# Window attention stage of a fused kernel: when the values are projected, in which PSUM bank, and the order of three small steps around it

## The chip, the cores and the metric

The kernel runs on one core of one Trainium2 chip. The metric is the device time of one execution in microseconds; lower is better. All times below are of the kernel before the change.

## The reference

Four images of 128 channels and 112 x 112 pixels pass two blocks with a residual each, `x = x + L0(gn(x))` and `x = x + L1(gn(x))`, where `gn` is a group norm over 32 groups of 4 channels. The change touches the first block only:

```python
win = (windows of 8 x 8 pixels: 64 tokens of 128 channels)
xn = (win - mu) * rsqrt(var + eps) * ln_gamma + ln_beta     # layer norm over the channels
q, k, v = split(xn @ w_qkv.T + b_qkv)                       # 8 heads of 16
attn = softmax((q * scale) @ k.T)                           # 64 x 64 for each window and head
o = (attn @ v) @ w_out.T + b_out
```

The second block is a linear attention over the whole image with a depthwise 3 x 3 convolution, and an MLP of 1024 hidden channels with the exact GELU. Its inputs need the group norm of what the first block wrote.

## The kernel before

All of it is one program. In the attention stage (the profile's first 1,080 us or so) an image of 112 x 112 lies in SBUF as `ximg` and is worked through in 14 strips of 8 rows, each of them 14 windows. A strip is two groups: `gg` = 0 with 4 pairs of windows (512 tokens) and `gg` = 1 with 3 pairs (384 tokens). Group number G runs from 0 to 111, even G has `gg` = 0. `group_loop` (L309) writes, for each engine, the prologue, then for each image strip 0 by itself, strips 1 to 11 in a hardware loop, and strips 12 and 13 by themselves. Each engine has its own `step` with its own written order; semaphores that count groups tie them together. There is no scheduler: the order in `step` is the order of execution.

The work on one group stretches over several steps (a pipeline written out by hand). In the step of group G:

- TensorE (L1379): `score_rows(G)` makes bf16 scores for the maxima; `out_transpose(G-2)`; `attend(G-1, h)` multiplies the probabilities with the values `vx`, half `h` = 1 (the pairs from the third on) into bank 7 and half 0 into bank 6; `ln_transpose(G+2)` and `ln_back(G+2)` turn the layer norm's input and output in bank 5; `out_project(G-2)` in bank 4; `transpose_maxima(G)` into the end of bank 6; `project_q(G+1)` into bank 7 and `project_k(G+1)` into bank 4; `score_cols(G)` makes the f32 scores, less the maxima, in the four banks `quad_banks`; `project_v(G+1)` into bank 7.
- VectorE (L1029): `maxima(G)`, `normalise(G-1, 1)` (softmax denominators, `oh`), `ln_stats(G+2)`, `mt_evac(G)`, `ln_moments(G+2)`, `normalise(G-1, 0)`, in odd groups `strip_stats` (statistics of the finished strip for the second group norm), `ln_norm(G+2)`, `v_evac(G+1)` (bank 7 to `vx`), and in even groups `next_stats` (statistics of a strip of the next image, which SyncE loads into `xs`; not in the last image).
- ScalarE (L692): `ot_evac(G-2)`, `ob_evac(G-2)`, `gn_apply(G+3)`, `q_evac(G+1)`, `k_evac(G+1)`, `exps(G)`, `xn_evac(G+2)`.
- GpSimd (L555): `xn_low(G+1)`, `residual(G-2)`, `ln_rstd(G+2)` (variance plus epsilon to the power -1/2, two instructions), `cast_q(G+1)`, `cast_k(G+1)` (bf16 copies for `score_rows` of the next step).
- SyncE stores the finished strip, reloads its place with the next image, and loads `xs`.

At strip 12 the steps also hold the group means and variances for the next image, at strip 13 the folding of weights. The rest of the kernel (second block) is not changed.

Of the kernel before, what the change touches and what calls it, by code (L numbers as in the profile page):

```python
# [30 lines left out]
P = 128  # L31
NIMG, C, H, W = 4, 128, 112, 112
HW = H * W
WIN, NH, HD = 8, 8, 16
# [7 lines left out]
QUADS = 4  # L42
# [8 lines left out]
GN_STRIP = 12  # L51
# [26 lines left out]
def build(nc, x_d, vec_d, fc1b_d, dw_d, wm_d, cm_d, w1_d, w2_d, sel_d, out_d):  # L78
    with ExitStack() as ctx:
# [74 lines left out]
        xn = sb("xn", [P, 2, 512], F32, stack_b)  # L154
# [36 lines left out]
        bank = [quad_banks[:, n, :] for n in range(QUADS)] + \  # L191
# [140 lines left out]
        def strip_back(i, s):  # L332
            return (i - 1, STRIPS - 1) if isinstance(s, int) and s == 0 else (i, s - 1)
# [154 lines left out]
        def _(pool):  # L488
# [33 lines left out]
            def xn_low(G, gg):  # L522
                n = P * GROUP_PAIRS[gg]
                pool.wait_ge(xn_ready, G + 1)
                g.tensor_tensor(xns[1][:, gg, 0:n], xn[:, gg, 0:n], xns[0][:, gg, 0:n].bitcast(F32),  # L525
                                ALU.subtract).then_inc(xnl_ready, 1)
# [28 lines left out]
            def step(G, i, s, gg, near):  # L555
                ng = 1 - gg
                if near(1):
                    xn_low(G + 1, ng)
                if near(-2):
                    residual(G - 2, strip_back(i, s)[1], gg)  # L560
                if near(2):
                    ln_rstd(G + 2, gg)
                if near(1):
                    cast_q(G + 1, ng)
                    cast_k(G + 1, ng)
                if at_norms(i, s) and gg == 0:
                    gn_coef(i + 1, norms_at(i))
# [252 lines left out]
        def _(dve):  # L820
# [130 lines left out]
            def v_evac(G, gg):  # L951


                n = GROUP_PAIRS[gg]
                dve.wait_ge(v_mm, G + 1)
                for e in range(2):
                    src = bank[7][64 * e:64 * e + 64, 0:P * n].rearrange("p (w j d) -> p w j d", j=QUADS, d=HD)
                    m = d.tensor_copy(vx[64 * e:64 * e + 64, gg, 0:2 * n, :, (HD + 1) * e:(HD + 1) * e + HD], src)  # L958
                m.then_inc(v_ready, 1)

# [45 lines left out]
            def next_stats(i, n):  # L1006

                dve.wait_ge(xs_loaded, (i * STRIPS + n + 1) * 16)
                hold(dve)
                bn_halves(lambda h: gst1[:, bass.ds(n * 2 + h, 1), :].rearrange("p a c -> p (a c)"), xs)\  # L1010
                    .then_inc(xs_done, 1)

            def strip_stats(i, s, done):

                dve.wait_ge(x1_ready, done)
                hold(dve)
                bn_halves(lambda h: gst2[:, i % 2, bass.ds(s * 2 + h, 1), :].rearrange("p a c -> p (a c)"),
                          ximg[:, bass.ds(s * STRIP, STRIP)]).then_inc(x1_summed, 1)

            def prologue():  # L1020
                ln_stats(0, 0)
                ln_moments(0, 0)
                ln_norm(0, 0)
                ln_stats(1, 1)
                ln_moments(1, 1)
                ln_norm(1, 1)
                v_evac(0, 0)

            def step(G, i, s, gg, near):  # L1029
                ng = 1 - gg  # L1030
                norms = at_norms(i, s) and gg == 0
                if norms and i == 0:
                    late_scale()
                if norms:
                    norm_moments(norms_at(i))
                maxima(G, gg)
                if near(-1):
                    normalise(G - 1, ng, 1)
                if near(2):
                    ln_stats(G + 2, gg)  # L1040
                if norms:
                    norm_spread(i + 1, norms_at(i), 6)
                mt_evac(G, gg)
                if norms:
                    norm_variance(i + 1, norms_at(i), 6)
                if i + 1 < NIMG and isinstance(s, int) and s == 0:
                    next_stats(i, gg)
                if near(2):
                    ln_moments(G + 2, gg)
                if near(-1):  # L1050
                    normalise(G - 1, ng, 0)
                if gg == 1 and near(-2):
                    strip_stats(*strip_back(i, s), G - 1)
                if near(2):
                    ln_norm(G + 2, gg)
                if near(1):
                    v_evac(G + 1, ng)
                if i + 1 < NIMG:
                    if gg == 0 and not (isinstance(s, int) and (s == 0 or s >= GN_STRIP)):
                        next_stats(i, s + 2)  # L1060
                    if gg == 1 and isinstance(s, int) and s == 0:
                        next_stats(i, 2)
                if gg == 1 and i == 0 and isinstance(s, int) and s == STRIPS - 1:
                    late_low()
                if gg == 1 and i > 0 and isinstance(s, int) and s == STRIPS - 1:
                    dve.wait_ge(gcoef_ready, i + 2)
                    fold_norm(i - 1)
# [177 lines left out]
        def _(pe):  # L1245
# [50 lines left out]
            def project_v(G, gg):  # L1296


                for w in range(2 * GROUP_PAIRS[gg]):
                    for e in range(2):  # L1300
                        m = mm(bank[7][64 * e:64 * e + 64, 64 * w:64 * w + 64], xn[:, gg, 64 * w:64 * w + 64],  # L1301
                               wvs[:, e, :], start=True, stop=True)
                m.then_inc(v_mm, 1)

# [4 lines left out]
            def score_rows(G, gg, reuse):  # L1309


                pe.wait_ge(q16_ready, G + 1)
                pe.wait_ge(k16_ready, G + 1)
                if reuse:
                    pe.wait_ge(prob_ready, G)
                for w in range(2 * GROUP_PAIRS[gg]):
                    t, w2 = w // 2, w % 2
                    for j in range(QUADS):
                        m = mm(bank[j][64 * w2:64 * w2 + 64, P * t:P * t + P], q16[quad_rows(j), gg, w, :],  # L1319
                               k16[quad_rows(j), gg, w, :, :].rearrange("p s k -> p (s k)"), start=True, stop=True)  # L1320
                m.then_inc(smax_mm, 1)
# [33 lines left out]
            def out_transpose(G, gg):  # L1355
                pe.wait_ge(oh_ready[0], G + 1)
                pe.wait_ge(oh_ready[1], G + 1)
                for t in range(GROUP_PAIRS[gg]):
                    m = tr(bank[4][:, P * t:P * t + P], oh[:, gg, P * t:P * t + P], cmat("ident"))
                m.then_inc(ot_mm, 1)  # L1360
# [6 lines left out]
            def prologue():  # L1367
                ln_transpose(0, 0)
                ln_back(0, 0)
                pe.wait_ge(xn_ready, 1)  # L1370
                ln_transpose(1, 1)
                pe.wait_ge(xnl_ready, 1)
                project_q(0, 0)
                project_k(0, 0)
                pe.wait_ge(q_ready, 1)
                project_v(0, 0)
                ln_back(1, 1)

            def step(G, i, s, gg, near):  # L1379
                ng = 1 - gg  # L1380
                norms = at_norms(i, s) and gg == 0
                score_rows(G, gg, near(-1))
                if near(-2):
                    out_transpose(G - 2, gg)
                pe.wait_ge(v_ready, G + 1)
                if near(-1):
                    attend(G - 1, ng, 1)
                if near(2):
                    pe.wait_ge(xn_ready, G + 2)
                    ln_transpose(G + 2, gg)  # L1390
                if near(-2):
                    out_project(G - 2, gg)
                if near(-1):
                    attend(G - 1, ng, 0)
                if norms:
                    group_means(i + 1, norms_at(i), 6)
                    group_variances(i + 1, norms_at(i), 6)
                transpose_maxima(G, gg)
                if near(1):
                    pe.wait_ge(xnl_ready, G + 2)  # L1400
                    if near(-1):
                        pe.wait_ge(oh_ready[1], G)
                    project_q(G + 1, ng)
                    if near(-2):
                        pe.wait_ge(ob_ready, G - 1)
                    project_k(G + 1, ng)
                score_cols(G, gg)
                if near(1):
                    pe.wait_ge(q_ready, G + 2)
                    project_v(G + 1, ng)  # L1410
                if near(2):
                    ln_back(G + 2, gg)

# [241 lines left out]
```

## Time and profile before

| | us |
|---|---|
| median of 3 runs | 2625.9 (2620.97 to 2631.47) |
| the profiled execution | 2624.75 |
| its span | 2623.0, mean granted TensorE clock 0.985 |
| TensorE busy | 2475.6 (94%) |
| VectorE busy | 2101.6 (80%) |
| ScalarE busy | 2138.7 (82%) |
| GpSimd busy | 1715.5 (65%) |

The span is the time from the first to the last instruction. Busy time counts instructions that compute; waits for semaphores are not in it. TensorE's ends are modelled and overlap the next start a little, so that its gaps are read best from start to start. A bracket behind a row gives the idle time before it and what released it.

### The profile page before, as it was taken

How to read it: one execution, taken by the hardware profiler on the slowest of the kernel's cores; microseconds unless marked ns; L12 is line 12 of the kernel's file. 1: busy time of each engine (PE TensorE's matmuls, PEld its weight loads, DVE VectorE, ACT ScalarE, POOL GpSimd, SP SyncE). 2: the span in 40 equal slices, each digit the busy share in tenths (PEclk: the TensorE clock that was granted, in tenths of full speed). 3: DMA queues.
4: the chain of work that ended last, by engine and by line, in shares of the span. 5: the costliest groups of instructions: out<-in, count | busy, mean ns of one | idle time of the engine just before them, and what ended most of it. 6: DMA issues, size and time to landing. Idle time of an engine off the chain costs nothing.

```text
span 2623.0 us, 111004 instructions
## 1 busy us (share of the span) xinstructions
PE 2475.6 (94%) x45772; PEld 2095.5 (80%) x45772; DVE 2101.6 (80%) x4316; ACT 2138.7 (82%) x3757; POOL 1715.5 (65%) x1714
## 2 busy tenths in 40 slices
PE   3999799989998999899899999999999999999999
PEld 2677567766776777798788989889898898988988
DVE  6888688878887888667778888888888888888885
ACT  2777577767776777566599999999999999999998
POOL 2555455545555555566477777777777777777778
PEclk9999899999999999999999999999999999999999
DMA  4222122212221111244301011110111111100000
GB/s 153 72 84 77 45 91 72 80 57 93 77 70 53 51 56 56 88 138 122 91 29 42 31 42 43 39 42 32 42 43 39 42 35 39 43 25 21 21 18 25
DMA packets 55799, 152.27 MB, mean 58 GB/s; under 512 B 6608, under 2 KB 20944, under 8 KB 55632
## 3 DMA queue, kind: packets, MB, share of 16 engines
q1 hardware_dynamic: 55632, 149.93, 17.5%
q8 instruction: 119, 1.95, 0.3%
q14 instruction: 48, 0.39, 0.0%
HBM read 98.52 MB, written 51.38 MB: 57 GB/s over the span
## 4 chain that ended last, share of the span: by engine, by line
PE 80%; DVE 10%; ACT 3%; issue 3%; POOL 3%; DVEq 0%; DMA 0%; SPq 0%; POOLq 0%; ACTq 0%
PE bank L1282 10%; PE bank L1284 9%; PE bank L1283 9%; PE quad_banks L1282 8%; PE quad_banks L1284 8%; PE quad_banks L1283 8%; PE quad_banks L1339 4%; PE quad_banks L1440 3%; PE bank L1507 3%; DVE mx L965 3%; PE bank L1440 3%; PE bank L1350 2%; PE bank L1365 2%; PE bank L1301 2%; DVE gst L827 2%
## 5 line engine op out<-in xcount | busy, mean ns | idle before, releaser
L606 POOL TENSOR_TENSOR hl<-hf,hh 128x448 fp32r<-128x448 f32 x896 | 1025.2, 1155 | 308.0 <-ACT hf L788 301.9
L787 ACT ACTIVATE hh<-quad_banks,fc1i 128x448 fp32r<-128x448 f32 x896 | 583.8, 652 | 67.6 <-PE quad_banks L1284 61.9
L1165 DVE SCALAR_TENSOR_TENSOR bank<-oring,dw,bank 128x448 f32<-128x448 f32 x896 | 615.1, 687 | 20.0
L788 ACT ACTIVATE hf<-quad_banks,fc1i 128x448 f32<-128x448 f32 x896 | 585.0, 653 | 0.0
L1282 PE MATMUL quad_banks<-t1h,w_hi 128*128 128x448 f32 x896 | 365.7, 408 | 5.6 <-DVE t1l L1184 5.6
L1282 PE MATMUL bank<-hh,w_hi 128*128 128x448 f32 x896 | 328.2, 366 | 0.0
L1284 PE MATMUL bank<-hl,w_hi 128*128 128x448 f32 x896 | 327.9, 366 | 0.0
L1284 PE MATMUL quad_banks<-t1l,w_hi 128*128 128x448 f32 x896 | 327.7, 366 | 0.0
L1283 PE MATMUL bank<-hh,w_lo 128*128 128x448 f32 x896 | 327.3, 365 | 0.0
L1283 PE MATMUL quad_banks<-t1h,w_lo 128*128 128x448 f32 x896 | 326.8, 365 | 0.0
L525 POOL TENSOR_TENSOR xn_lo<-xn,xn_hi 128x512 fp32r<-128x512 f32 x112 | 128.9, 1151 | 246.8 <-ACT xn_hi L644 246.8
L553 POOL TENSOR_TENSOR ximg<-ximg,ob 128x512 f32 (+1 forms) x112 | 127.9, 1142 | 168.8 <-ACT ob L679 168.8
L965 DVE TENSOR_REDUCE mx<-quad_banks 128x32 bf16<-128x2048 f32 x112 | 226.8, 2025 | 12.6 <-PE quad_banks L1319 9.6
L666 ACT ACTIVATE prob<-quad_banks 128x2048 f32<-128x2048 f32 x112 | 186.4, 1664 | 52.0 <-PE quad_banks L1339 51.3
L1350 PEld LDWEIGHTS bank<-vx,prob 128*32 128x32 f32 x12544 | 131.9, 110 | 102.0 <-issue 91.0
L1282 PEld LDWEIGHTS quad_banks<-t1h,w_hi 128*128 128x128 f32 x896 | 168.8, 188 | 39.0 <-issue 26.5
L1283 PEld LDWEIGHTS quad_banks<-t1h,w_lo 128*128 128x128 f32 x896 | 168.8, 188 | 32.3 <-issue 20.4
L958 DVE COPY vx<-bank 64x512 f32<-64x512 f32 x224 | 139.0, 621 | 64.6 <-PE bank L1301 63.0
L1170 DVE TENSOR_TENSOR dwl<-bank,dwh 128x448 fp32r<-128x448 f32 x112 | 70.0, 625 | 144.5 <-ACT dwh L774 144.5
L947 DVE TENSOR_SCALAR xc<-bank,lnmv,lnrs 128x128 f32<-128x128 f32 x392 | 134.5, 403 | 60.9 <-POOL lnrs L519 60.9
L1284 PEld LDWEIGHTS bank<-hl,w_hi 128*128 128x128 f32 x896 | 168.3, 188 | 14.3
L1284 PEld LDWEIGHTS quad_banks<-t1l,w_hi 128*128 128x128 f32 x896 | 168.6, 188 | 13.4
(186 smaller groups left out, 5864.7 us busy)
## 6 DMA issues: line engine op xcount, KB each, us to landing
ximg<-x SPq DMA_DIRECT2D x112, 448.0 KB, 3.4
ximg<-x_in SPq DMA_DIRECT2D x56, 448.0 KB, 3.4
x<-ximg SPq DMA_DIRECT2D x56, 448.0 KB, 2.5
y_out<-yb SPq DMA_DIRECT2D x112, 224.0 KB, 1.9
xs<-x_in SPq DMA_DIRECT2D x42, 448.0 KB, 3.3
wm<-wm_in SPq DMA_DIRECT2D x1, 512.0 KB, 5.2
w1f<-w_in SPq DMA_DIRECT2D x1, 512.0 KB, 8.6
w<-w_in SPq DMA_DIRECT2D x1, 512.0 KB, 9.6
```

The costliest lines, as they stand in the source:

```text
L606: g.tensor_tensor(hl[:, k, :], hf[:, k, :], hh[:, k, :].bitcast(F32), ALU.subtract).then_inc(hl_ready, 1)
L666: a.activation(prob[:, :, 0:n // 64].rearrange("p j w q -> p j (w q)"), quad_banks[:, :, 0:n], ACT.Exp)\
L787: a.activation(hh[:, j, :], p, ACT.Gelu, bias=bias)
L788: a.activation(hf[:, j, :], p, ACT.Gelu, bias=bias).then_inc(hf_ready, 1)
L958: m = d.tensor_copy(vx[64 * e:64 * e + 64, gg, 0:2 * n, :, (HD + 1) * e:(HD + 1) * e + HD], src)
L965: d.tensor_reduce(dst, quad_banks[:, :, 0:P * n].rearrange("p j (e k) -> p j e k", k=64), AX.X, ALU.max)\
L1165: m = d.scalar_tensor_tensor(acc, src, dw[:, k:k + 1], acc, ALU.mult, ALU.add)
L1282: mm(out, w[0], x[0], start=start, stop=False)
L1283: mm(out, w[1], x[0], start=False, stop=False)
L1284: return mm(out, w[0], x[1], start=False, stop=stop)
L1350: m = mm(bank[6 + h][32 * q:32 * q + 32, c:c + VCOLS], prob[:, j, w, 32 * (q % 2):32 * (q % 2) + 32], vx[:, gg, w, j, :], start=True, stop ...
L1440: m = mm(bank[2 + cc][:, 2 * P * t:2 * P * t + 2 * P], x[:, sp, c], w.rearrange("p a b -> p (a b)"), start=(k == 0), stop=(k == 2))
```

## The change

Four edits, in the attention stage alone.

1. The values of group G are projected in the step of G rather than G-1, by `project_v(G)` at the same place of TensorE's step and `v_evac(G)` at the same place of VectorE's; the pair of prologue calls goes. So the step of an even group has the four-pair values and that of an odd group the three-pair ones, the reverse of before. They go into bank 6 and not 7. The wait for `q_ready` goes, a wait for `oh_ready[0]` of G-1 comes. `attend(G-1)` waits for `v_ready` of G-1.
2. In odd groups `out_transpose(G-2)` comes before `score_rows(G)`, with a wait for `k_ready` (both use bank 4).
3. On VectorE `next_stats` of the even groups moves ahead of `ln_norm`.
4. On GpSimd `ln_rstd(G+2)` of the even groups moves ahead of `residual(G-2)`.

```diff
--- before.py
+++ after.py
@@ -556,9 +556,11 @@
                 ng = 1 - gg
                 if near(1):
                     xn_low(G + 1, ng)
+                if gg == 0 and near(2):
+                    ln_rstd(G + 2, gg)
                 if near(-2):
                     residual(G - 2, strip_back(i, s)[1], gg)
-                if near(2):
+                if gg == 1 and near(2):
                     ln_rstd(G + 2, gg)
                 if near(1):
                     cast_q(G + 1, ng)
@@ -954,7 +956,7 @@
                 n = GROUP_PAIRS[gg]
                 dve.wait_ge(v_mm, G + 1)
                 for e in range(2):
-                    src = bank[7][64 * e:64 * e + 64, 0:P * n].rearrange("p (w j d) -> p w j d", j=QUADS, d=HD)
+                    src = bank[6][64 * e:64 * e + 64, 0:P * n].rearrange("p (w j d) -> p w j d", j=QUADS, d=HD)
                     m = d.tensor_copy(vx[64 * e:64 * e + 64, gg, 0:2 * n, :, (HD + 1) * e:(HD + 1) * e + HD], src)
                 m.then_inc(v_ready, 1)
 
@@ -1024,7 +1026,6 @@
                 ln_stats(1, 1)
                 ln_moments(1, 1)
                 ln_norm(1, 1)
-                v_evac(0, 0)
 
             def step(G, i, s, gg, near):
                 ng = 1 - gg
@@ -1051,15 +1052,13 @@
                     normalise(G - 1, ng, 0)
                 if gg == 1 and near(-2):
                     strip_stats(*strip_back(i, s), G - 1)
+                if i + 1 < NIMG and gg == 0 and not (isinstance(s, int) and (s == 0 or s >= GN_STRIP)):
+                    next_stats(i, s + 2)
                 if near(2):
                     ln_norm(G + 2, gg)
-                if near(1):
-                    v_evac(G + 1, ng)
-                if i + 1 < NIMG:
-                    if gg == 0 and not (isinstance(s, int) and (s == 0 or s >= GN_STRIP)):
-                        next_stats(i, s + 2)
-                    if gg == 1 and isinstance(s, int) and s == 0:
-                        next_stats(i, 2)
+                v_evac(G, gg)
+                if i + 1 < NIMG and gg == 1 and isinstance(s, int) and s == 0:
+                    next_stats(i, 2)
                 if gg == 1 and i == 0 and isinstance(s, int) and s == STRIPS - 1:
                     late_low()
                 if gg == 1 and i > 0 and isinstance(s, int) and s == STRIPS - 1:
@@ -1298,7 +1297,7 @@
 
                 for w in range(2 * GROUP_PAIRS[gg]):
                     for e in range(2):
-                        m = mm(bank[7][64 * e:64 * e + 64, 64 * w:64 * w + 64], xn[:, gg, 64 * w:64 * w + 64],
+                        m = mm(bank[6][64 * e:64 * e + 64, 64 * w:64 * w + 64], xn[:, gg, 64 * w:64 * w + 64],
                                wvs[:, e, :], start=True, stop=True)
                 m.then_inc(v_mm, 1)
 
@@ -1372,18 +1371,21 @@
                 pe.wait_ge(xnl_ready, 1)
                 project_q(0, 0)
                 project_k(0, 0)
-                pe.wait_ge(q_ready, 1)
-                project_v(0, 0)
                 ln_back(1, 1)
 
             def step(G, i, s, gg, near):
                 ng = 1 - gg
                 norms = at_norms(i, s) and gg == 0
-                score_rows(G, gg, near(-1))
+                if gg == 0:
+                    score_rows(G, gg, near(-1))
                 if near(-2):
+                    if gg == 1:
+                        pe.wait_ge(k_ready, G + 1)
                     out_transpose(G - 2, gg)
-                pe.wait_ge(v_ready, G + 1)
+                if gg == 1:
+                    score_rows(G, gg, near(-1))
                 if near(-1):
+                    pe.wait_ge(v_ready, G)
                     attend(G - 1, ng, 1)
                 if near(2):
                     pe.wait_ge(xn_ready, G + 2)
@@ -1405,9 +1407,9 @@
                         pe.wait_ge(ob_ready, G - 1)
                     project_k(G + 1, ng)
                 score_cols(G, gg)
-                if near(1):
-                    pe.wait_ge(q_ready, G + 2)
-                    project_v(G + 1, ng)
+                if near(-1):
+                    pe.wait_ge(oh_ready[0], G)
+                project_v(G, gg)
                 if near(2):
                     ln_back(G + 2, gg)
```

## Rows read from the trace of the kernel before

**Rows 1.** Stretches between even groups' maxima: start:end, length, busy time (instructions), clock, DMA

```profile
88.20:245.40 157.20, 149.75 (x5644) 113.66 (x5643) 139.15 (x370) 120.87 (x163) 87.89 (x108) 1.00 0.24 79
245.40:356.16 110.76, 93.41 (x3140) 70.44 (x3139) 84.85 (x222) 70.41 (x101) 51.18 (x62) 0.89 0.21 65
...
616.04:773.10 157.06, 149.56 (x5644) 113.53 (x5643) 139.49 (x369) 120.74 (x163) 87.85 (x108) 1.00 0.24 79
...
873.54:1027.12 153.58, 147.91 (x5643) 112.84 (x5643) 129.51 (x351) 120.77 (x163) 87.64 (x108) 1.00 0.16 54
...
sum 1015.56, PE 934.31 PEld 709.82 DVE 852.97 ACT 739.42 POOL 540.80; mean PE 103.81 PEld 78.87 DVE 94.77 ACT 82.16 POOL 60.09
```

**Rows 2.** TensorE's timeline, one strip of image 1: start us, length, engine, line

```profile
501.77 0.92 PE L1301 MATMUL bank<-wvs,xn 128*64 128x64 f32 x24
...
503.90 0.37 PE L1319 MATMUL quad_banks<-k,q 32*64 32x128 bf16 x24 [0.32 <-ACT prob L666]
...
504.68 0.77 PE L1350 MATMUL bank<-vx,prob 128*32 128x34 f32 x64
...
505.76 0.81 PE L1365 MATMUL bank<-ot,wm 128*128 128x384 f32 x2
...
507.20 0.23 PE L1325 MATMUL bank<-ident,mx 128*128 128x128 bf16 x1
507.65 0.47 PE L1282 MATMUL bank<-xn_hi,pw_hi 128*128 128x512 f32 x1 [0.22 <-DVE oh L981]
...
510.65 1.15 PE L1301 MATMUL bank<-wvs,xn 128*64 128x64 f32 x32
...
513.30 0.47 PE L1350 MATMUL bank<-vx,prob 128*32 128x34 f32 x32
...
515.94 0.23 PE L1325 MATMUL bank<-ident,mx 128*128 128x128 bf16 x1
516.15 0.41 PE L1282 MATMUL bank<-xn_hi,pw_hi 128*128 128x384 f32 x1
...
519.22 0.92 PE L1301 MATMUL bank<-wvs,xn 128*64 128x64 f32 x24
```

**Rows 3.** TensorE's timeline in image 3, odd group's transposed maxima and query projection

```profile
936.13 0.23 PE L1325 MATMUL bank<-ident,mx 128*128 128x128 bf16 x1
936.17 0.48 PE L1282 MATMUL bank<-xn_hi,pw_hi 128*128 128x512 f32 x1
```

**Rows 4.** VectorE's timeline of the same strip as rows 2

```profile
501.50 1.37 DVE L947 TENSOR_SCALAR xc<-bank,lnmv,lnrs 128x128 f32<-128x128 f32 x4 [1.02 <-POOL lnrs L519]
...
505.12 1.76 DVE L965 TENSOR_REDUCE mx<-quad_banks 128x24 bf16<-128x1536 f32 x1
...
507.08 0.42 DVE L981 TENSOR_TENSOR oh<-bank,rden 128x256 f32<-128x256 f32 x1
...
509.10 1.15 DVE L827 BATCH_NORM_STATS2 gst<-ximg  x2
...
511.85 1.39 DVE L958 COPY vx<-bank 64x512 f32<-64x512 f32 x2 [0.65 <-PE bank L1301]
513.27 2.29 DVE L965 TENSOR_REDUCE mx<-quad_banks 128x32 bf16<-128x2048 f32 x1
...
516.95 0.38 DVE L940 BATCH_NORM_AGGREGATE lnmv<-lnst 128x2 f32<-128x6 f32 x4
```

**Rows 5.** ScalarE's timeline of that strip, odd group's `ot`

```profile
504.98 0.59 ACT L674 ACTIVATE ot<-bank,vec 128x384 f32<-128x384 f32 x1
```

**Rows 6.** GpSimd's timeline of that strip

```profile
509.08 0.88 POOL L519 TENSOR_TENSOR lnrs<-lnve,neghalf 128x3 f32<-128x3 f32 x1
...
516.32 1.27 POOL L553 TENSOR_TENSOR ximg<-ximg,ob 128x512 f32 x1 [1.69 <-ACT ob L679]
517.56 0.23 POOL L517 TENSOR_SCALAR lnve<-lnmv 128x4 f32<-128x4 f32 x1
...
519.32 0.83 POOL L533 CAST k<-kx 128x768 bf16<-128x768 f32 x1
```

## The prediction

> **What bounds the kernel now.** I read the busy table first (TensorE 94%), then the windows of the attention stage, the only stage the change touches. It is a chain of strips, each an even group of four window pairs and an odd one of three. [rows 1] cut the stage at the starts of the even groups' maxima. In images 0 to 2 there are three stretches of nine strips, the first and the last shown, at 157.1 to 157.2 us, 17.46 a strip; in image 3, nine strips at 153.58, 17.06 a strip. The other 19 of the 55 periods lie around image changes, 1015.56 − 3·157.1 − 153.6 = 391 us, 20.6 each. All steady stretches are granted 1.00 of the clock.
>
> Then I read one steady strip of TensorE [rows 2]. The reader is to see that it never rests for long, yet the strip holds four short waits. Two are before `score_rows` (L1319) for the exponentials, and in the odd one it is 0.32; two are before the query projection (L1282) for a DVE `oh` tile. Starts lie about 0.07 closer than the modelled ends, so a wait is best taken from start to start: the transposed maxima cost 0.04 where nothing waits (936.13 to 936.17, where L1282 has no idle bracket) [rows 3], but L1282 comes 0.45 after them in the odd group and 0.21 in the even one. The strip splits into four edges:
> - A, end of the even `score_cols` (start of L1301, 501.77) to the odd group's first `attend` (504.68): 2.91.
> - D, from there to the end of the odd `score_cols` (510.65): 5.97, of which 0.41 is the wait at L1282.
> - B, to the even group's `attend` (513.30): 2.65.
> - C, to the even `score_cols`' end (519.22): 5.92, 0.17 of it wait.
> Sum 17.45. Image 3, which has no statistics of a next image, loses the 0.41 in D and so has 17.05.
>
> **Edge A: transposition first, values a group later.** Today's order in A is values (three pairs), `ln_back`, `score_rows`, `out_transpose`. The start of `score_rows` is set by the exponentials, 503.90 − 501.77 = 2.13 after the scores; it stays there. From it to `attend` are 0.78 (503.90 to 504.68): 0.30 for itself (its 0.37 less the overlap of 0.07) and 0.48 for `out_transpose`. After the change `out_transpose` sits in front, inside that wait, so by the exponentials `attend` could start at 2.13 + 0.30 = 2.43. But it now needs this strip's four-pair values: from the start of such a projection to the start of DVE's copies 511.85 − 510.65 = 1.20, the copies 1.39 [rows 4], and the release to TensorE. The last is 0.15 from `oh` to L1282 (507.08 + 0.42 against 507.65) [rows 2, 4] and at the least nothing; I take 0.10. A becomes 2.69, saving 0.22; it is bound by the copies, not the exponentials. `ln_back`'s own wait lies inside A and is not counted again.
>
> **Edge B.** In B the order is unchanged (the transposition moves in odd groups alone). The shorter three-pair values make more room for the exponentials, that is all: `score_rows` waits for them as before, so 2.65 stays. Moving the V weights' work from one group to the other removes none: 24 + 32 products before and after.
>
> **Edge C.** `oh` for L1282 comes at the end of maxima, reciprocal, product on DVE. The even maxima start now at 513.27, 2.62 after the odd scores' end, because DVE is at the four-pair copies until then. After the change it has the three-pair copies (about 0.28 less), and the scores themselves become the release: `attend` at 2.65 less at most 0.64 for the four transposed tiles (0.48·4/3) is 2.01, with 0.16 to 0.2 for the release about 2.2. From maxima to L1282 it is 516.15 − 513.27 = 2.88 [rows 2, 4], so the query could start at 5.1. TensorE gets there at 2.65 + (515.94 − 513.30) + 0.04 = 5.33. The wait of 0.17 goes, with 0.2 to spare.
>
> **Edge D, and the statistics moved up.** In images 0 to 2 the odd maxima start late because DVE does `ln_norm`, copies, and only then `next_stats`, as long as the other statistics pair (1.15) [rows 4]; ahead of `ln_norm` it had idled 1.02 (501.50) for the reciprocal deviation. After the change the statistics stand in that idle time. Then the copies end at 1.20 + 1.39 = 2.59 after the even scores, maxima follow at 2.62, and 507.65 − 505.12 = 2.53 later the query may start: 5.15. TensorE reaches it at 2.69 + (507.20 − 504.68) + 0.04 = 5.25, 5.34 with the next item. So the 0.41 goes. Next late there: `ot`. ScalarE ends it at 504.98 + 0.59 [rows 5], 3.80 after the even scores; `out_project` would like to start at 2.69 + (505.76 − 504.68) = 3.77, and a 0.06 release gives a new wait of 0.09.
>
> **The variance root moved up (even groups).** GpSimd today does the residual (1.27) and then the root, which starts at 517.56 [rows 6]; the moments end at 516.95 + 0.38 = 517.33 [rows 4], so at present the move would win only the 0.03 to 0.1 above a release of 0.2. But moments will come earlier (even maxima 0.4 earlier), and then the residual, which waits for `ob`, would be in the way. Counting from the odd scores' end: maxima 2.2, moments + 4.06 = 6.3, root starts at 6.5 and ends at 7.8. DVE has `oh` done at 6.9, statistics to 8.05, `ln_norm` (1.37) to 9.45, release 0.06: 9.5, against the even values' end at 2.65 + 5.75 + 1.08 = 9.48. `ln_back` then waits for nothing, or 0.02. The price is paid by what is queued behind the root: residual, cast of q, cast of k, which the odd `score_rows` awaits. From the root's start to the k cast's end is 519.32 + 0.83 − 517.56 = 2.59, plus about 1.25 for the residual: 6.5 + 3.85 = 10.35, with a release 10.45 to 10.5. The exponentials allow `score_rows` at 2.65 + 5.75 + 2.13 = 10.53. It fits with nearly nothing to spare, but 0.25 more is free, since `attend` waits for the copies. In odd groups nothing moves on GpSimd.
>
> **Waits added.** `project_v` waits for the even or odd `oh` half that frees bank 6: DVE ends it over 1 us ahead (half 0 lies ahead of the statistics at 509.10, the values start at 510.65), so nothing. `k_ready` before the odd transposition: ScalarE writes it before it starts the exponentials, nothing. No DMA is moved; the load of the statistics strip is started by `next_stats`' end, 2 us earlier and with the same period, so SP's queue has the same 17 us for it.
>
> **Sum.** After: A 2.69 + D 5.97 − 0.41 + 0.09 + B 2.65 + C 5.92 − 0.17 = 16.74, in both kinds of strip. Images 0 to 2: 27·(17.46 − 16.74) = 19.4; image 3: 9·(17.06 − 16.74) = 2.9. The 19 others: [rows 1] show the first image change with 0.89 of the clock and 93 of 111 us busy, held up by the norm's chain and by issue gaps that the change leaves alone. There the saving is between 0 and, with every term, 0.72: 0 to 13.7. I take 0.35, the middle (the same waits for `oh` and the exponentials occur there, but in about half of the groups something longer hides them): 6.6. The first projection leaves the prologue and one more stands at the end: nothing. Total 28.9. Against the profiled execution, 2624.75 with a span of 2623.0, this gives 2596; the median of the three runs is 2625.9, 1.2 higher, so 2597.
>
> Bounds for the strip: the release 0 to 0.15 moves A by ±0.1 at most; if DVE is 0.3 later than I figured (`next_stats` not wholly hidden), D or A grows by 0.3. That is 16.65 to 17.05 and, with the others' 0 to 13.7, 2583 to 2615.
>
> **A rule that speaks against it.** [rows 4, 6] show that a statistics pair on DVE (509.10, 1.15 long) and GpSimd's root (509.08) already run at the same time in odd groups, with the root at 0.88. The Trainium skill (SBUF — State Buffer, "Who interferes with whom") says DVE and GpSimd share one port pair as an exclusive lock, and that whoever issues first blocks the other for a whole instruction; it exempts a DVE instruction with one SBUF input outside the 2-port modes. By the lock without the exemption, the root would be held up by one statistics instruction; by this row it isn't, so the rule's exemption is the side that the trace supports.
>
> **Rivals.**
> 1. GpSimd's chain becomes the bound (slower). Place: even group, moments, root, residual, two casts, odd `score_rows`. It is free up to 0.3 later than figured (0.05 and the 0.25), and costs all beyond; at 1.0 later, the strips of images 0 to 2 are no faster than before, at 0.6 those of image 3. A root held up for two statistics instructions (1.15) would give 16.74 + 0.85 = 17.6 a strip: 27·0.14 + 9·0.54 = 8.6 more than before, 2634. For: the margin is nearly nothing. Against: the overlap at 509.1, and every duration in the chain has a row. 0.06.
> 2. DVE doesn't come free as figured, and half of the gain stays: its even list has no idle time left between `oh` and the copies, so 0.3 of lateness reaches `ln_back`, the copies and `attend`. 17.05 a strip: 27·0.41 = 11, others 3: 2612. 0.14.
> 3. The waits around image changes shrink as much as in steady strips: 2626 − 22.3 − 13.7 = 2590; with a release of nothing, 2585. 0.10.
> 4. The waits that go return elsewhere at once: exponentials (0.4 of waiting before `score_rows`, which the change doesn't touch) prove to set the whole strip, 2624 to 2628. For: they are in each group. Against: [rows 3] lose 0.41 of wait and the period falls by 0.40, so DVE's lateness does count. 0.07.
>
> **Chances.** Forecast 0.63, the others as given. What can be told from no change is 0.5%, 13 us: faster than 2613 takes the forecast, rival 3 and half of rival 2 and a bit more, 0.83; same 0.13, in which rival 1 lies too as priced; slower (over 2639) needs its lateness above 1.3, 0.04. The range that holds 8 in 10 is 2584 to 2614.
>
> **What would show it.** Steady strips at 16.7 to 16.8 in all four images, the same with and without next statistics. L1282 without an idle bracket in both groups. DVE's idle time before `ln_norm` near nothing in images 0 to 2 and about 1.0 in image 3. TensorE's first `attend` of odd groups released by the value copies. The k cast of even groups ending within 0.1 to 0.3 before the odd `score_rows`. If a new wait of TensorE for GpSimd's k cast over 0.3 appears, rival 1 is at work; a strip above 17.1 makes the forecast wrong.

## The result and the profile after

The changed kernel takes 2597.4 us (median of 4 runs, 2595.0 to 2598.3) against 2623.4 of the kernel before (4 runs, 2616.1 to 2631.5): ratio 0.9908, 95% interval 0.9892 to 0.9924. The forecast was 2597, range 2584 to 2614.

The stretches between even groups' maxima, as in [rows 1], cut at the same strips of the changed kernel:

```profile
90.24:241.76 151.52, 146.51 (x5645) 112.62 (x5646) 139.23 (x370) 120.89 (x163) 87.41 (x108) 1.00 0.25 82
241.76:350.03 108.27, 90.29 (x3141) 68.30 (x3141) 84.62 (x222) 70.30 (x101) 50.22 (x62) 0.92 0.21 67
...
753.92:847.45 93.53, 85.51 (x3140) 65.25 (x3140) 77.76 (x209) 67.34 (x91) 50.15 (x64) 0.98 0.16 53
847.45:999.61 152.16, 147.16 (x5644) 113.15 (x5644) 130.31 (x352) 120.79 (x163) 87.35 (x108) 1.00 0.16 54
...
sum 987.33, PE 916.72 PEld 702.70 DVE 854.06 ACT 738.35 POOL 536.66; mean PE 101.86 PEld 78.08 DVE 94.90 ACT 82.04 POOL 59.63
```

Steady strips fell from 17.46 to 151.5 / 9 = 16.83 us in images 0 to 2 and from 17.06 to 16.91 in image 3. That is 17.0 us in the first 27 strips and 1.4 in the nine others. The 19 periods around image changes fell from 390.6 to 380.8, and 6.9 of these 9.8 us lie in the third image change alone (93.53 now). The kernel before had there:

```profile
773.10:873.54 100.44, 88.28 (x3140) 67.22 (x3139) 77.50 (x209) 67.24 (x91) 50.42 (x64) 0.95 0.15 49
```

The stage is 28.2 us shorter, the span 26.5: the stage begins 0.7 later and the second block takes 1.1 more. Against the median shown with the prediction (2625.9) the changed kernel is 28.5 faster.

TensorE's timeline of a strip of image 1, to be held beside [rows 2]:

```profile
485.11 0.47 PE L1349 MATMUL bank<-vx,prob 128*32 128x34 f32 x32
...
487.72 0.23 PE L1324 MATMUL bank<-ident,mx 128*128 128x128 bf16 x1
487.76 0.42 PE L1281 MATMUL bank<-xn_hi,pw_hi 128*128 128x384 f32 x1
...
490.85 1.15 PE L1300 MATMUL bank<-wvs,xn 128*64 128x64 f32 x32
...
492.42 0.49 PE L1358 MATMUL bank<-cm,oh 128*128 128x128 f32 x3
492.98 0.37 PE L1318 MATMUL quad_banks<-k,q 32*64 32x128 bf16 x24
493.49 0.77 PE L1349 MATMUL bank<-vx,prob 128*32 128x34 f32 x64
494.30 0.54 PE L1270 MATMUL bank<-cm,xg 128*128 128x128 f32 x3
494.70 0.91 PE L1364 MATMUL bank<-ot,wm 128*128 128x384 f32 x2
...
496.24 0.23 PE L1324 MATMUL bank<-ident,mx 128*128 128x128 bf16 x1
496.28 0.48 PE L1281 MATMUL bank<-xn_hi,pw_hi 128*128 128x512 f32 x1
...
499.29 0.92 PE L1300 MATMUL bank<-wvs,xn 128*64 128x64 f32 x24
...
500.99 0.43 PE L1318 MATMUL quad_banks<-k,q 32*64 32x128 bf16 x32 [0.31 <-ACT prob L668]
```

Four things are to be seen. The query projection follows the transposed maxima by 0.04 in both groups, so both waits for `oh` are gone. `out_transpose` (492.42) lies ahead of the odd `score_rows`, which still starts 2.13 after the even scores' end (492.98 − 490.85). The first `attend` comes at 2.64. But `ln_transpose` follows it after 0.81, where before it was 0.70 (504.68 of [rows 2] to 505.38, in the line below), and `out_project` is 0.91 long against the 0.81 of [rows 2]: two waits that bear no bracket. The even `score_rows` starts 1.70 after the odd scores' end (500.99 − 499.29), as before (512.35 − 510.65), held by the exponentials; only the wait is longer, since three-pair values fill less of the time. From the trace of the kernel before:

```profile
505.38 0.55 PE L1271 MATMUL bank<-cm,xg 128*128 128x128 f32 x3
```

VectorE, to be held beside [rows 4]:

```profile
489.28 1.15 DVE L829 BATCH_NORM_STATS2 gst<-xs 128x448 f32 x2
490.35 1.35 DVE L949 TENSOR_SCALAR xc<-bank,lnmv,lnrs 128x128 f32<-128x128 f32 x4
492.05 1.39 DVE L960 COPY vx<-bank 64x512 f32<-64x512 f32 x2 [0.34 <-PE bank L1300]
493.47 1.76 DVE L967 TENSOR_REDUCE mx<-quad_banks 128x24 bf16<-128x1536 f32 x1
...
497.89 1.15 DVE L829 BATCH_NORM_STATS2 gst<-ximg  x2 [0.34 <-POOL ximg L553]
```

`next_stats` runs from 489.28 and `ln_norm` follows with no idle bracket where [rows 4] show 1.02. The odd maxima follow the value copies at once (493.47), and so does TensorE's first `attend` of the odd group: the copies end at 492.05 + 1.39 = 493.44, 0.05 before it. In image 3, where there are no statistics to fill it, the idle time before the even `ln_norm` is 0.98.

ScalarE, `xn`, `xn_hi` and `ot`, beside [rows 5]:

```profile
492.73 0.77 ACT L644 ACTIVATE xn<-bank,vec 128x512 f32<-128x512 f32 x1
493.39 0.78 ACT L646 ACTIVATE xn_hi<-bank,vec 128x512 fp32r<-128x512 f32 x1
494.06 0.59 ACT L676 ACTIVATE ot<-bank,vec 128x384 f32<-128x384 f32 x1
```

`xn_hi` ends at 494.17, 0.13 before `ln_transpose`; `ot` ends at 494.65, 0.05 before `out_project`'s row. Both follow the even exponentials without a gap.

GpSimd, root (its first instruction) and k cast of the even group, beside [rows 6]:

```profile
488.95 0.23 POOL L517 TENSOR_SCALAR lnve<-lnmv 128x4 f32<-128x4 f32 x1 [2.71 <-DVE lnmv L942]
...
491.93 0.83 POOL L533 CAST k<-kx 128x768 bf16<-128x768 f32 x1
```

The k cast ends at 492.76, 0.22 before the odd `score_rows`.

### The profile page after: what moved, and what is told of

Read it like the earlier page. It is cut to its first block, busy times and chain, and to the rows that moved or that the text cites. A ratio compares the mean times of both kernels' runs of the same rounds, so it can differ in the third digit from the quotient of the medians.

```text
span 2596.5 us, 111004 instructions
## 1 busy us (share of the span) xinstructions
PE 2459.1 (95%) x45772; PEld 2089.1 (80%) x45772; DVE 2102.8 (81%) x4316; ACT 2139.0 (82%) x3757; POOL 1712.4 (66%) x1714
## 3 DMA queue, kind: packets, MB, share of 16 engines
q1 hardware_dynamic: 55632, 149.93, 17.7%
## 4 chain that ended last, share of the span: by engine, by line
PE 84%; ACT 6%; DVE 6%; issue 3%; POOL 0%; DMA 0%; SPq 0%; DVEq 0%; POOLq 0%; ACTq 0%
PE bank L1281 10%; PE bank L1283 9%; PE bank L1282 9%; PE quad_banks L1281 8%; PE quad_banks L1283 8%; PE quad_banks L1282 8%; PE bank L1349 5%; PE quad_banks L1338 4%; PE bank L1364 3%; PE quad_banks L1442 3%; PE bank L1509 3%; PE bank L1300 3%; PE bank L1442 3%; ACT prob L668 2%; PE bank L1270 2%
## 5 line engine op out<-in xcount | busy, mean ns | idle before, releaser
L1282 PEld LDWEIGHTS bank<-hh,w_lo 128*128 128x128 f32 x896 | 168.3, 188 | 12.9
L1281 PEld LDWEIGHTS bank<-hh,w_hi 128*128 128x128 f32 x896 | 168.3, 188 | 12.8 <-POOL hl L608 0.4
```

The lines of the kernel that those rows point to most:

```text
L1281: mm(out, w[0], x[0], start=start, stop=False)
L1282: mm(out, w[1], x[0], start=False, stop=False)
```

## The experiments

Times are medians of 4 to 10 runs, and each ratio is to the kernel before as timed beside that run. The table gives the edges named in the prediction, from starts in TensorE's timeline (median of the strips of a stretch in image 1), the strip, image 3's strip, and the time.

| kernel | A | D | B | C | strip, images 0 to 2 | image 3 | median us | ratio (95%) |
|---|---|---|---|---|---|---|---|---|
| before | 2.91 | 5.97 | 2.65 | 5.92 | 17.46 | 17.06 | 2621 to 2623 | 1 |
| changed | 2.65 | 5.80 | 2.65 | 5.74 | 16.83 | 16.91 | 2597.4 | 0.9908 (0.9892 to 0.9924) |
| without statistics moved | 2.65 | 6.70 | 2.65 | 5.75 | 17.75 | 16.92 | 2626.3 | 1.001 (1.000 to 1.002) |
| statistics moved alone | 2.91 | 5.57 | 2.65 | 5.92 | 17.07 | 17.08 | 2613.6 | 0.9958 (0.9943 to 0.9972) |
| without transposition first | 2.91 | 5.59 | 2.65 | 5.74 | 16.89 | 17.07 | 2602.1 | 0.9915 (0.9899 to 0.9932) |
| without root moved | 2.65 | 5.91 | 2.65 | 5.75 | 16.94 | 17.00 | 2603.8 | 0.9927 (0.9910 to 0.9943) |
| without values' turn | 2.51 | 5.94 | 2.65 | 5.94 | 17.03 | 17.02 | 2604.7 | 0.9948 (0.9931 to 0.9965) |
| values' turn alone | 2.91 | 6.44 | 2.65 | 5.73 | 17.73 | 17.12 | 2627.1 | 1.0024 (1.0013 to 1.0035) |
| values in bank 7 | 2.65 | 5.79 | 2.65 | 5.74 | 16.83 | 16.91 | 2596.3 | 0.9912 (0.9895 to 0.9928) |
| transposition first in both | 2.65 | 5.79 | 2.35 | 6.13 | 16.92 | 16.93 | 2599.4 | 0.9916 (0.9897 to 0.9935) |
| and k first in even groups | 2.65 | 5.82 | 2.35 | 6.05 | 16.87 | 16.86 | 2598.9 | 0.9913 (0.9896 to 0.9929) |
| both halves of attend first | 2.65 | 5.53 | 2.91 | 5.80 | 16.86 | 16.90 | 2605.1 | 0.9936 (0.9920 to 0.9953) |

**The statistics put back.**

```diff
-                if i + 1 < NIMG and gg == 0 and not (...):
-                    next_stats(i, s + 2)
                 if near(2):
                     ln_norm(G + 2, gg)
                 v_evac(G, gg)
+                if i + 1 < NIMG and gg == 0 and not (...):
+                    next_stats(i, s + 2)
```

Expected: 

> The changed kernel with edit 3 undone: the even groups' next_stats stands behind the value copies again. Theory (VectorE's lateness for the odd maxima is what edit 3 removes): copies now hold four pairs and end 2.6 us after the even scores, the statistics (1.2) follow, so the odd maxima start at 3.8 and the odd query projection can start at 3.8 + 2.5 = 6.3, where TensorE is ready at 5.45: a new wait of 0.8 to 0.9. Strips of images 0 to 2: 17.6 to 17.7 us, longer than before the change (17.46); image 3, which has no next statistics, unchanged at 16.9. Whole: 27 x 0.8 + some 4 around image changes = 25 us over the changed kernel, about 2622, level with the kernel before. Rival (the gain is the values' turn, the place of the statistics matters little): strips at 16.9 to 17.0, 2600.

TensorE's timeline, a strip of image 0:

```profile
168.30 1.15 PE L1300 MATMUL bank<-wvs,xn 128*64 128x64 f32 x32
...
170.95 0.77 PE L1349 MATMUL bank<-vx,prob 128*32 128x34 f32 x64
...
173.92 0.23 PE L1324 MATMUL bank<-ident,mx 128*128 128x128 bf16 x1 [0.17 <-DVE mx L967]
174.63 0.47 PE L1281 MATMUL bank<-xn_hi,pw_hi 128*128 128x512 f32 x1 [0.48 <-DVE oh L983]
```

Measured 17.75 a strip and 2626.3, where the theory had 17.6 to 17.7 and about 2622: right in kind, 4 us short in the whole. The rows name the late one: the transposed maxima wait for VectorE's maxima and the query projection for `oh`. Image 3 has no such statistics and keeps 16.92. The rival falls.

**The statistics moved alone.** The kernel before with edit 3 only, the same lines moved.

Expected: 

> The kernel before with edit 3 alone. Theory: the wait of 0.41 for oh before the odd query projection goes in images 0 to 2 and nothing else: 17.05 to 17.10 us a strip there, 17.06 in image 3 as before. 27 x 0.40 = 10.8 plus 1 to 3 around image changes: 2610 to 2613, ratio to before 0.995. Rival: no gain without the values' turn, 17.4 a strip, ratio 0.999 to 1.001.

17.07 in images 0 to 2 and 17.08 in image 3, 2613.6: edge D alone shrank, by 0.40. Here too the rival falls.

**The transposition put back behind `score_rows`.**

```diff
-                if gg == 0:
-                    score_rows(G, gg, near(-1))
+                score_rows(G, gg, near(-1))
                 if near(-2):
-                    if gg == 1:
-                        pe.wait_ge(k_ready, G + 1)
                     out_transpose(G - 2, gg)
-                if gg == 1:
-                    score_rows(G, gg, near(-1))
```

Expected: 

> The changed kernel with edit 2 undone (odd score_rows before out_transpose). Theory: edge A is then 2.13 + 0.30 + 0.48 = 2.91 instead of 2.64, but edge D gives back the two short waits for ScalarE's xn and ot (5.80 to about 5.6), so a strip costs 16.90 to 16.95 against 16.83, in all four images: 3 to 5 us more, 2601. Rival (the transposition first is worth all of its 0.48 in the wait): 17.1 a strip or more, 2607 or more.

TensorE's timeline, image 0 (values, `score_rows`, `attend`, `ln_transpose`):

```profile
164.78 1.15 PE L1300 MATMUL bank<-wvs,xn 128*64 128x64 f32 x32
...
166.91 0.37 PE L1318 MATMUL quad_banks<-k,q 32*64 32x128 bf16 x24 [0.39 <-ACT prob L668]
...
167.69 0.77 PE L1349 MATMUL bank<-vx,prob 128*32 128x34 f32 x64
168.39 0.55 PE L1270 MATMUL bank<-cm,xg 128*128 128x128 f32 x3
```

A is 0.26 longer and D 0.21 shorter. `ln_transpose` comes 3.61 after the even scores, against 3.45 in the changed kernel, and neither item waits any more: `ln_transpose` is 0.70 behind `attend` again (167.69 to 168.39) and `out_project` 0.81 long. So the edit that fills a 0.4 us wait with 0.48 us of work is worth 0.06 a strip in images 0 to 2. In image 3 it is 0.16, because there B is 0.1 longer without it (the even `score_rows` takes 0.55 to the next item instead of 0.45), which I can't explain (see the last section). So the 16.90 to 16.95 expected in all four images holds for images 0 to 2 (16.89) and is missed in image 3. The whole time, 4.7 us up, is no more than the two intervals leave open.

**The root put back behind the residual.**

```diff
-                if gg == 0 and near(2):
-                    ln_rstd(G + 2, gg)
                 if near(-2):
                     residual(...)
-                if gg == 1 and near(2):
+                if near(2):
                     ln_rstd(G + 2, gg)
```

Expected: 

> The changed kernel with edit 4 undone (residual before the root in even groups). Theory: from the odd scores' end ob is out at 5.4, residual 5.7 to 6.95, root to 8.25, ln_norm to 9.65, so ln_back waits about 0.2 but the value copies start only 0.05 later: 16.88 to 16.95 a strip, 1 to 4 us more, 2599 to 2601. Rival (GpSimd's order was needed for the gain): ln_back's wait goes in full to the strip, 17.05 or more, 2605 or more.

TensorE's timeline, image 0:

```profile
164.47 1.15 PE L1298 MATMUL bank<-wvs,xn 128*64 128x64 f32 x32
165.75 0.66 PE L1274 MATMUL bank<-cm,xc 128*128 128x128 f32 x4
...
167.12 0.77 PE L1347 MATMUL bank<-vx,prob 128*32 128x34 f32 x64
168.02 0.54 PE L1268 MATMUL bank<-cm,xg 128*128 128x128 f32 x3
```

ScalarE there:

```profile
166.45 0.78 ACT L642 ACTIVATE xn<-bank,vec 128x512 f32<-128x512 f32 x1
```

The strip, 16.94, is at the expected place, but the way there differs. `ln_back` starts 1.28 after the even values' start (1.08 in the changed kernel), the value copies cost nothing more (A is 2.65), and the loss stands in D: ScalarE's `xn` starts at 1.98 instead of 1.88, which I read as a wait for `ln_back`, since the exponentials had been what held it before, and `ln_transpose` is 0.90 behind `attend` instead of 0.81. The time rose by 6 us, more than the 36 strips explain (4 us).

**The values a group earlier again.** The kernel before with edits 2, 3 and 4.

Expected: 

> The kernel before with edits 2, 3 and 4, so the changed kernel without edit 1 (values of G+1 in G's step, bank 7). Theory (edit 1 is worth little more than the wait before the even query projection, because VectorE has three-pair copies ahead of the even maxima): edge C is 5.92 again, edge A is set by the k cast behind the residual, 2.13 + 0.17 + 0.30 = 2.60, D 5.80, B 2.65: 16.95 us a strip (16.83 in the changed kernel), 2601 to 2603. Rival (edit 1 carries the gain): 17.2 or more a strip, 2611 or more.

TensorE's timeline, image 0:

```profile
160.81 0.92 PE L1302 MATMUL bank<-wvs,xn 128*64 128x64 f32 x24
...
163.32 0.77 PE L1351 MATMUL bank<-vx,prob 128*32 128x34 f32 x64
164.26 0.54 PE L1272 MATMUL bank<-cm,xg 128*128 128x128 f32 x3 [0.18 <-ACT xn_hi L646]
...
169.25 1.15 PE L1302 MATMUL bank<-wvs,xn 128*64 128x64 f32 x32
```

Strip 17.03, 2604.7: nearer to the theory's 16.95 and 2601 to 2603 than to the rival's 17.2 and 2611, and the whole miss is in edge D, 5.94 for 5.80. It shows more: `attend` now comes at 2.51, 0.14 before that of the changed kernel, and `ln_transpose` at 164.26 − 160.81 = 3.45, exactly where the changed kernel has it (494.30 − 490.85 = 3.45). A + D is 8.45 in both. So the wait for the value copies, which bounds edge A, costs the changed kernel nothing: here the row itself names what `ln_transpose` waits for, ScalarE's `xn_hi`. What edit 1 brings is edge C alone, 0.18 to 0.20.

**The values' turn alone.** The kernel before with edit 1 only.

Expected: 

> The kernel before with edit 1 alone. Theory: four-pair copies now stand ahead of the statistics and both ahead of the odd maxima, which start at 3.8 after the even scores: the query projection can start at 6.33, TensorE is ready at 2.91 + 2.56 = 5.47, so D becomes 6.4; A 2.91, B 2.65, C 5.75: 17.7 us a strip in images 0 to 2, against 17.46 before; 16.9 to 17.1 in image 3. Whole: some 7 us slower than before, 2630. Rival (edit 1 carries the gain): faster than before, 17.1 or less a strip.

17.73 a strip and 2627.1: alone, the values' turn makes the kernel slower by 0.24% (0.13 to 0.35%), since the four-pair copies join the statistics ahead of the odd maxima.

**The values in bank 7.**

```diff
-    src = bank[6][...]                       # v_evac, and the matmul likewise
+    src = bank[7][...]
...
-                if near(-1):
-                    pe.wait_ge(oh_ready[0], G)
+                if near(1):
+                    pe.wait_ge(q_ready, G + 2)
+                else:
+                    pe.wait_ge(oh_ready[1], G)
                 project_v(G, gg)
```

Expected: 

> The changed kernel with the values of G in G's step but in bank 7 again, with the old wait for q_ready in place of that for oh_ready[0]. Theory: neither wait is ever the last, and attend(G) in bank 7 waits for the copies anyway for their data, so the bank is worth nothing: 16.83 a strip, 2597, within 2 us. Rival (the bank frees TensorE or VectorE): 17.0 or more a strip, 2603 or more.

16.83, 16.91 and 2596.3: the bank is worth nothing.

**The transposition first in even groups too.** `if near(-2): wait k_ready; out_transpose(...)` and then `score_rows` in every group.

Expected: 

> The changed kernel with out_transpose ahead of score_rows in even groups too. Theory: the wait of 0.4 to 0.5 for the exponentials before the even score_rows takes the transposition in, so attend comes at 2.2 to 2.3 instead of 2.65 after the odd scores, but the maxima start 0.12 later and ScalarE's xn is not out yet at the layer norm's transposition (a wait of some 0.2) and VectorE's oh again a little: 0.1 to 0.15 of 0.47 stay, 16.7 a strip, 2592 to 2595. Rival (each 0.1 off the wait goes to the strip): 16.4, 2582.

TensorE's timeline of image 1, even query projection, then the turn from an odd to an even group:

```profile
488.04 0.23 PE L1324 MATMUL bank<-ident,mx 128*128 128x128 bf16 x1
488.37 0.41 PE L1281 MATMUL bank<-xn_hi,pw_hi 128*128 128x384 f32 x1
...
500.74 0.55 PE L1276 MATMUL bank<-cm,xc 128*128 128x128 f32 x3
501.32 0.63 PE L1358 MATMUL bank<-cm,oh 128*128 128x128 f32 x4
501.88 0.32 PE L1318 MATMUL quad_banks<-k,q 32*64 32x128 bf16 x16
```

The same turn one strip on, into strip 12, which is written out behind the hardware loop:

```profile
517.68 0.55 PE L1276 MATMUL bank<-cm,xc 128*128 128x128 f32 x3
518.06 0.60 PE L1358 MATMUL bank<-cm,oh 128*128 128x128 f32 x4
```

Both the theory's 16.7 and the rival's 16.4 were wrong; it is 16.92, no better than without. Even `score_rows` starts at 1.99, not at the 1.76 that work alone allows: `out_transpose` starts 0.58 behind `ln_back`'s first tile, where three tiles take 0.38 (517.68 to 518.06). The trace says where the 0.2 belongs. The distance is 0.54 to 0.64 in strips 3 to 11 of every image, where the hardware loop turns between the two items, and 0.38 or 0.39 in strips 12, 13 and 0 of the later images, which are written out by themselves; in strips 12 and 13 `score_rows` starts at 1.76 or 1.77. In these strips the loop's turn is what differs, so I read it as costing TensorE some 0.2 that no wait covers in this form. The expectation did not have it, and it is about what the strip lacks of 16.7; that it would be 16.7 without it is argued and not shown. The maxima move with it, and the query projection waits 0.29 (0.33 less 0.04). B gained 0.30, C lost 0.39.

**k ahead of q in even groups**, on TensorE, ScalarE and GpSimd, on top of that.

```diff
+                    if gg == 0: (wait ob_ready) project_k(G + 1, ng)
                     (wait oh_ready[1]) project_q(G + 1, ng)
+                    if gg == 1: (wait ob_ready) project_k(G + 1, ng)
```

Expected: 

> transpose_first_both with k ahead of q in the even groups (project, evacuate and cast k of G+1, then q). There the even query projection waited 0.34 for VectorE's oh in bank 7, which gave back what the transposition had taken from the exponentials' wait. Theory: k (bank 4) needs only ob, out 0.12 after TensorE is ready; q then comes 0.6 later and waits for nothing. Edge C 6.13 to about 5.9, strip 16.92 to 16.65 or 16.70: 2590. Rival (VectorE's chain from maxima to the transposed maxima is itself the cycle, so the wait only moves to score_cols): 16.9 a strip, 2599.

16.87 instead of 16.65 to 16.70: nearer to the rival's 16.9. C gave back 0.08 of 0.39. The k projection waits 0.20 for `ob` in the place of the query's 0.29 for `oh`, so the two are late together.

**Both halves of `attend` first in odd groups.**

```diff
                     attend(G - 1, ng, 1)
+                if gg == 1 and near(-1):
+                    attend(G - 1, ng, 0)
                 if near(2): ... ln_transpose(G + 2, gg)
                 if near(-2): out_project(G - 2, gg)
-                if near(-1):
+                if gg == 0 and near(-1):
                     attend(G - 1, ng, 0)
```

Expected: 

> The changed kernel with both halves of attend ahead of ln_transpose and out_project in odd groups. Theory (the 0.2 by which edge D is longer than its work is TensorE waiting for ScalarE's xn_hi and ot): with 0.70 of attend in front, both are out in time; attend to the odd scores' end falls from 5.80 to 5.6 unless the key projection waits for ob, which comes 0.5 to 0.6 later. The later ob moves residual, strip statistics and ln_norm, so 0.1 to 0.2 comes back before the even score_rows and query: 16.75 to 16.85 a strip, 2594 to 2598. Rival (the 0.2 is the cost of TensorE's own order of banks): 5.8 stays.

TensorE's timeline, `ln_back` of an odd group, then edges A and D:

```profile
487.12 0.55 PE L1276 MATMUL bank<-cm,xc 128*128 128x128 f32 x3 [0.43 <-DVE xc L949]
...
494.45 1.15 PE L1300 MATMUL bank<-wvs,xn 128*64 128x64 f32 x32
...
497.10 1.33 PE L1349 MATMUL bank<-vx,prob 128*32 128x34 f32 x128
498.36 0.55 PE L1270 MATMUL bank<-cm,xg 128*128 128x128 f32 x3
...
502.61 0.57 PE L1300 MATMUL bank<-wvs,xn 128*64 128x64 f32 x12
```

VectorE there, odd group:

```profile
501.83 1.15 DVE L829 BATCH_NORM_STATS2 gst<-ximg  x2 [0.70 <-POOL ximg L553]
```

D falls to 5.53 (5.51 in the strip shown), although the query projection now waits 0.17 for `oh`. The theory's reading, that the surplus of D was TensorE's wait for `xn_hi` and `ot`, fits. But this form can't prove it alone, for the order itself is shorter on TensorE: the two halves, `ln_transpose` and `out_project` take 2.29 from first start to the transposed maxima, against 2.75 in the changed kernel and 2.52 in the form with the transposition put back, which has the changed kernel's order of these items and no wait among them. It is that form, and the bracket on `xn_hi` in the form without the values' turn, that show the 0.23 to be waiting. The price is there too: `out_project` is later, so `ob`, residual and strip statistics (0.70 of idle for GpSimd's residual, 0.34 in the changed kernel), and `ln_back` of the odd group waits 0.43 for `xc`. B grows by 0.26. The strip is level (16.86, the end of the range 16.75 to 16.85 that was expected); the whole is 8 us longer than the changed kernel, since the periods around image changes (390.7) lose what the changed kernel had gained there (380.8). Why these periods differ by 10 us between kernels with the same steady strips wasn't settled; the granted clock in them is lower here than in the changed kernel in two of five stretches and higher in none (0.96, 0.92, 0.92, 0.98, 1.00 against 1.00, 0.92, 0.98, 0.98, 1.00).

## Why the prediction was right, step by step

- **Edges D and C, the two `oh` waits.** Right. C is 5.74 where 5.75 was worked out. The statistics put back bring the whole wait in D back and more; moved alone they take 0.40 of the 0.63 won per strip in images 0 to 2. Beside the other edits their place is worth more, 0.92 (17.75 against 16.83): the values' turn without it is slower than before.
- **Edge A.** `attend` came at 2.65 where 2.69 was figured, and the copies do release it. But as a gain this step failed. The prediction took the 0.22 of A as won and put only 0.09 against it in D. Two kernels (the changed one and that without the values' turn) show that `ln_transpose` stands at 3.45 after the even scores whether `attend` comes at 2.51 or at 2.65, and one of them names ScalarE's `xn_hi` in its bracket. With `attend` at 2.91 (transposition put back) the wait is gone. That chain (exponentials 1.88, `xn`, `xn_hi`, `ot`, back to back) was in the trace of before; the prediction looked only at its last member. The new waits are 0.11, 0.02 and 0.10 (before `ln_transpose`, before `out_project` and within it), so D is 5.80, not 5.65, and A and D together gained 0.43 of a forecast 0.54. To this extent rival 4, waits that return elsewhere at once, came true beside the forecast.
- **Edge B.** Right, 2.65 in images 0 to 2. In image 3 it is 2.73, so the strips are not the same with and without next statistics, as the prediction had said they would be.
- **The variance root.** The placement of the root and of the casts was right within 0.1 (`ln_norm` ended 0.2 earlier than figured): the k cast ends at 491.93 + 0.83 − 482.46 = 10.30 after the odd scores (482.46 is 485.11 − 2.65), against 10.35 figured, and never holds `score_rows` up. Rival 1 did not come. The edit is worth 0.1 a strip, but by another way than I gave: it lets `ln_back` end before ScalarE is free.
- **Sum.** Strips 16.83 and 16.91 against 16.74. 27·0.09 + 9·0.17 = 4 us less gained than forecast; around image changes 9.8 were gained and 6.6 forecast. With the 1.8 lost outside the stage, 26.5 of 28.9: that the time was met so closely is in part luck, two errors of 4.0 and 3.2 us with opposite sign. The 6.6 was the middle of a range and no run shows it; of the 9.8, most lies in one image change, where the granted clock was higher as well (0.98 against 0.95), and each kernel has one trace of it. The lower bound doesn't follow from its own terms: a strip of 16.65 and 13.7 for the others save 27·0.81 + 9·0.41 + 13.7 = 39.3, which gives 2587 and not 2583.
- **The values' bank** was counted at nothing and is nothing.

No form that was tried was faster than the changed kernel: the bank-7 form (2596.3) is level with it, and the times do not settle the order among the forms within some 5 us, whose intervals overlap. What bounds a strip now is TensorE's own work (146.5 us busy of the 151.5 of nine strips) with three releases that move against each other: ScalarE's exponentials (2.13 and 1.70 after the scores), its `xn`/`ot` behind them, and VectorE's maxima.

## What to carry to other kernels

Write the strip as a cycle of edges between two or three anchor instructions, taken start to start, and for each edge list every chain that ends in it, not only the one that the profile names: the chain behind it took back 0.2 of the 0.26 us here. Where work stands on its engine matters only if others wait for what is queued behind it: the same 1.15 us of statistics cost 0.4 us behind the copies and nothing ahead of `ln_norm`. Edits made together can be worth more than their parts: the values' turn alone cost 0.27 a strip, and beside the moved statistics it was worth 0.20.

## What the runs showed of the hardware

- The turn of a hardware loop can cost TensorE 0.2 us. With the transposition first in both, the item after the turn starts 0.54 to 0.64 behind `ln_back`'s first tile in strips 3 to 11 of all images and 0.38 or 0.39 in strips 12, 13 and 0, where nothing turns; between the same two items of the odd step, inside the loop's body, four tiles are 0.49 apart, as long as they take. The form with k first shows the same (0.55 to 0.63 against 0.38 or 0.39). The first turn of each loop, into strip 2, is not like the others: 0.38, 0.38, 0.43 and 0.66 in the four images. In the changed kernel the even `score_rows` starts at 1.70 or 1.71 in strips 3 to 12 alike, held by the exponentials, so the turn is hidden there.
- The even `score_rows` isn't always paced evenly, and the turn of the loop alone doesn't explain it. In image 3 of the changed kernel its 32 products take 0.44 to 0.46 to the next item in strips 3 to 11 where those of image 1 take 0.36, with one start 0.08 late among them. Of that image's strips written out by themselves, 0 and 13 take 0.59 and 0.63 and strip 12 takes 0.40, and strips 6 to 11 of image 0 take 0.47 to 0.50 with the statistics moved alone, while the kernel before has 0.36 throughout image 3. The cause stays open.
- GpSimd's root (1.03) and VectorE's statistics (1.15) now run side by side in even groups (489.26 and 489.28), each as long as apart: in image 3, with no statistics beside it, the even root is 1.03 too, and in the kernel before, where the same statistics stood behind the value copies, they took 1.15. No blocking shows, as the row of the odd group had promised.
- All steady stretches are granted 1.00 of TensorE's clock before and after. The five stretches around them have 0.91, 0.89, 0.95, 0.95 and 1.00 before and 1.00, 0.92, 0.98, 0.98 and 1.00 after. The kernels differ by up to 13 us in these 19 periods (378.6 to 391.3) without a pattern that follows the edits. The clock is no full answer: the shortest, with the values in bank 7, has 0.91, 0.94, 0.95, 0.98 and 0.95 there, less than the changed kernel with 380.8.
